# Four stacked graph layers on one core: a group's chain, weighing, sums and 11 of its 16 adds put into one slot, the rest into the next

## The reference

```
L0: msgs = edge_weight * h[src];  agg = segment_sum(msgs, dst);  leaky_relu((agg + h) @ W1.T + agg*h @ W2.T + b)
L1: a = <q[src], k[dst]> / sqrt(32) in 4 heads;  softmax over the edges of a dst;  agg = sum(sa * v[src]);  gate, norm
L2: two GATv2 layers (4 heads, then 1):  score = att . leaky_relu(xl[src] + xr[dst]);  softmax;  sum(alpha * xl[src])
L3: two typed layers (8 heads, 8 node types, 8 edge types):  a = <Watt k[src], q[dst]>;  softmax;  sum(alpha * Wmsg v[src])
```

## Time and profile before

| what | value |
| --- | --- |
| median of three runs | 6962.94 us |
| the profiled execution | 6951.92 us |
| its span | 6950.0 us |
| PE busy | 4911.1 us, 71% |
| DVE busy | 4761.2 us, 69% |
| POOL busy | 4755.9 us, 68% |
| ACT busy | 1562.0 us, 22% |
| mean granted PE clock | 0.786 |

### The profile page before, as it was taken

The page is one execution under the profiler, slowest core; times in us unless marked ns, Lnnn a source line. Parts: engine busy times, 40 slices in busy tenths (PEclk is TensorE's granted clock), DMA queues, the critical chain, the costliest instruction groups (busy, mean ns, idle before and its releaser), DMA issues. The chain is left out here.

```text
span 6950.0 us, 92236 instructions
## 1 busy us (share of the span) xinstructions
PE 4911.1 (71%) x26631; PEld 4085.5 (59%) x26631; DVE 4761.2 (69%) x14309; ACT 1562.0 (22%) x4929; POOL 4755.9 (68%) x5008
## 2 busy tenths in 40 slices
PE   2655555667766577777688888867888886667766
PEld 2444444556665465565466666656777775566665
DVE  4444443777877577877577777747777874788786
ACT  2433332222222111111112112111222221121121
POOL 3777776777776577777577666627777763777774
PEclk8666666777677788888799889968887886877776
DMA  4444445666666355555455555547766673666664
GB/s 133 165 164 158 159 164 146 204 216 210 214 217 180 125 161 167 166 155 167 121 171 179 167 164 175 168 121 228 242 229 229 231 219 134 215 226 220 223 226 138
DMA packets 408006, 1267.81 MB, mean 182 GB/s; under 512 B 128774, under 2 KB 189958, under 8 KB 321110
## 3 DMA queue, kind: packets, MB, share of 16 engines
q1 hardware_dynamic: 200000, 760.73, 30.7%
q0 software_dynamic: 200240, 496.31, 25.8%
q10 hardware_dynamic: 7270, 4.88, 0.3%
HBM read 1084.56 MB, written 176.98 MB: 182 GB/s over the span
## 5 line engine op out<-in xcount | busy, mean ns | idle before, releaser
L756 POOL DMA_INDIRECT gathered_rows<-table_l,arena x3056 | 2909.3, 952 | 1192.4 <-issue 904.2
L1298 PE MATMUL ps<-weighted_rows,onehot 128*128 128x136 f32 (+2 forms) x8320 | 1527.4, 341 | 573.9 <-DVE acc L1150 568.8
L1298 PEld LDWEIGHTS ps<-weighted_rows,onehot 128*128 128x128 f32 x8320 | 1353.3, 241 | 729.3 <-DVE weighted_rows L1139 334.1
L1260 PEld LDWEIGHTS ps<-dst_side,onehot_t 128*128 128x128 f32 x8320 | 1299.9, 232 | 384.1 <-issue 318.3
L756 POOL DMA_INDIRECT gathered_rows<-table_l,src_rel_edges x1120 | 1063.7, 950 | 603.5 <-issue 328.4
L1260 PE MATMUL ps<-dst_side,onehot_t 128*128 x8320 | 1381.4, 320 | 90.0 <-DVE products L1067 43.8
L1150 DVE TENSOR_TENSOR acc<-acc,ps 128x136 f32 (+2 forms) x4160 | 1185.9, 285 | 178.1 <-PE ps L1298 83.5
L1256 PE MATMUL ps<-gathered_rows,ident 128*128 128x512 f32 x832 | 547.3, 745 | 307.0 <-DMA gathered_rows<-table_l,arena 302.4
L1072 DVE TENSOR_REDUCE scores<-products 128x16 f32<-128x512 f32 (+2 forms) x1040 | 706.5, 679 | 10.0
L879 PE MATMUL ps<-gathered_rows,onehot 128*128 128x128 f32 x1664 | 346.3, 373 | 465.3 <-ACT gathered_rows L816 464.3
L756 POOL DMA_INDIRECT arena<-table_l,src_rel_edges x544 | 516.5, 950 | 180.2 <-issue 160.3
(11 more groups left out here) (322 smaller groups left out, 6029.5 us busy)
## 6 DMA issues: line engine op xcount, KB each, us to landing
onehot_t<-onehots_turned SPq DMA_DIRECT2D x260, 1024.0 KB
onehot<-onehots SPq DMA_DIRECT2D x260, 1024.0 KB
onehots<-onehot SPq DMA_DIRECT2D x52, 1024.0 KB, 6.8
onehots_turned<-onehot_t SPq DMA_DIRECT2D x52, 1024.0 KB, 4.3
table_l<-arena SPq DMA_DIRECT2D x50, 1024.0 KB
gathered_rows<-table_l,arena POOLq DMA_INDIRECT x3056, 2.5
segment_flags_sb<-segment_flags SPq DMA_DIRECT2D x1300, 8.2 KB
arena<-type_mask_rows SPq DMA_DIRECT2D x75, 256.0 KB
```

The source lines that it names most:

```text
L756: pool.indirect_dma_start(out=home(v, t // GC)[:, t % GC, :], out_offset=None, in_=table, in_offset=bass.IndirectOffsetOnAxis(ap=index[:, ...
L1260: ins = nc.tensor.matmul(ps[:, BZ + k, g * P:(g + 1) * P], e.ohT[:, u, t * P:(t + 1) * P], kRows[:, bass.ds(bs[t % 8], D)], start=not gat, ...
L1298: ins = nc.tensor.matmul(ps[:, BP + n % 3, at:at + PW], e.oh[:, u, t, :], exvT[:, t, :], start=True, stop=True)
```

## The change

VectorE's slot s now does, in this order: the last five adds of group s-2 around the scans of group s-1; the whole chain of s-1, with `product(s, 0)` and `score(s, 0)` in it; then a wait for the exponentials' columns of s-1 and its weighing; then the products and scores 1 to 3 of s with the first 11 adds (units 0 to 3) of s-1 between them. TensorE makes all four `dst_rows` of group s in slot s; those of chunks 2 and 3 stand behind `sums` 3 and 5. In the GAT passes the identity product comes after the four one-hot products instead of before them. There is one slot less at the end of a pass, and `first(k)` is 9 hooks earlier for blocks whose last tile is one of the first 8 or last 5 of its group (for tiles 8 to 10 it is 11 earlier). GpSimd does not gather the last two tiles, which hold no edges, and the waits on gathered rows are for that many fewer.

```diff
+ON_TIME = SUMMED[3][1]
...
+def rows_wanted(s, j, q):
+    return 64 * (q + 1) - (16 * LACK if s == NG - 1 and j == J - 1 else 0)
...
-            for t in range(GT):
+            for t in range(min(GT, NT_MAX - s * GT)):
...
# VectorE, slot(s): r = s - 1, o = s - 2
+                if late:
+                    bo = blocks_of(o, ON_TIME, GT - ON_TIME)
+                    unit_of_adds(o, 4, ON_TIME, bo)
                 if chain:
                     scan_tiles(r, v, rq)
+                if late:
+                    unit_of_adds(o, 5, ON_TIME, bo)
                 if chain:
                     turn_ends(r)
+                after.dve(dve, x)
                 after.dve(dve, x + 1)
...
                 if chain:
                     chain_backward(r, v)
                     hand_back_ends(r)
+                    open_drop(r)
+                    max_forward(r, v)
+                    max_backward(r, v)
+                    less_maximum(r)
+                if cur:
+                    score(s, 0)
                 after.dve(dve, x + 2)
                 if chain:
+                    e.excol_ready.wait(dve, a_no, r + 1)
+                    last_maxima(r)
+                    for j in range(J):
+                        weigh(r, (w - 1) % buffers, j)
+                    br = blocks_of(r, 0, ON_TIME)
+                    rescale(r, v, br[0])
                 after.dve(dve, x + 3)
                 if cur:
                     product(s, w, qw, 1)
                     score(s, 1)
+                if chain:
+                    unit_of_adds(r, 0, 0, br)
                 after.dve(dve, x + 4)
+                if chain:
+                    unit_of_adds(r, 1, 0, br)
                 after.dve(dve, x + 5)
                 if cur:
                     product(s, w, qw, 2)
                     score(s, 2)
+                if chain:
+                    unit_of_adds(r, 2, 0, br)
+                    unit_of_adds(r, 3, 0, br)
                 after.dve(dve, x + 6)
                 if cur:
                     product(s, w, qw, 3)
                     score(s, 3)
...
# TensorE, slot(s)
+                if chain:
+                    turn_scores(r)
                 after.pe(pe, x)
+                if cur:
+                    e.oht_here[u].wait(pe, a_no, 16 * (q + 1))
+                    dst_rows(s, w, qw, 0, bs)
+                after.pe(pe, x + 1)
+                if chain:
+                    spread_drop(r)
+                after.pe(pe, x + 2)
+                if chain:
+                    turn_back(r)
+                if cur:
+                    dst_rows(s, w, qw, 1, bs)
+                after.pe(pe, x + 3)
+                if chain:
+                    e.oh_here[v].wait(pe, a_no, 16 * (rq + 1))
+                    for n in range(3):
+                        sums(r, v, n)
...
+                after.pe(pe, x + 4)
+                if chain:
+                    sums(r, v, 3)
+                after.pe(pe, x + 5)
+                if cur:
+                    dst_rows(s, w, qw, 2, bs)
+                if chain:
+                    sums(r, v, 4)
+                    sums(r, v, 5)
+                after.pe(pe, x + 6)
+                if cur:
+                    dst_rows(s, w, qw, 3, bs)
                 after.pe(pe, x + 7)
...
-        return HOOKS * (s + 2) + 7 if t < 8 else HOOKS * (s + 3) + 1
+        return HOOKS * (s + 1) + 6 if t < ON_TIME else HOOKS * (s + 2)
```

More of the change, by code:

```diff
@@ L1047, in _ @@
             slot(NG, NG % ways, NG // ways, cur=False)
-            slot(NG + 1, (NG + 1) % ways, (NG + 1) // ways, cur=False, chain=False)
-            for x in range(HOOKS * (NG + 2), after.end):
+            for x in range(HOOKS * (NG + 1), after.end):
                 after.act(act, x)
@@ L1235, in _ @@
             for s in range(ways):
-                slot(s, s, 0, chain=s > 0, weighs=s > 1, late=s > 2)
+                slot(s, s, 0, chain=s > 0, late=s > 1)
             turns(slot, ways, NG, ways)
-            for n in range(3):
-                slot(NG + n, (NG + n) % ways, (NG + n) // ways, cur=False, chain=n < 1, weighs=n < 2)
-            for x in range(HOOKS * (NG + 3), after.end):
+            slot(NG, NG % ways, NG // ways, cur=False)
+            slot(NG + 1, (NG + 1) % ways, (NG + 1) // ways, cur=False, chain=False)
+            for x in range(HOOKS * (NG + 2), after.end):
                 after.dve(dve, x)
@@ L1331, in slot @@
                     dst_rows(s, w, qw, 3, bs)
-                after.pe(pe, x + 5)
-                after.pe(pe, x + 6)
-                if weighs:
-                    sums(p, u, 4)
-                    sums(p, u, 5)
-                if chain:
-                    turn_back(r)
-                if cur and ahead:
-                    un, un_q = two(wn, qn)
-                    e.oht_here[un].wait(pe, a_no, 16 * (un_q + 1))
-                    bn = blocks_of(s + 1, 0)
-                    dst_rows(s + 1, wn, qn, 0, bn)
@@ L1344, in slot @@
-                after.pe(pe, x + 7)
-                if cur:
-                    turn_scores(s)
-                if cur and ahead:
-                    dst_rows(s + 1, wn, qn, 1, bn)
-            e.oht_here[0].wait(pe, a_no, 16)
-            b0 = blocks_of(0, 0)
-            for j in range(2):
-                dst_rows(0, 0, 0, j, b0)
+                after.pe(pe, x + 7)
             for s in range(ways):
-                slot(s, s, 0, chain=s > 0, weighs=s > 1)
-            turns(slot, ways, NG - 1, ways)
@@ L1357, in _ @@
-            slot(NG - 1, (NG - 1) % ways, (NG - 1) // ways, ahead=False)
+                slot(s, s, 0, chain=s > 0)
+            turns(slot, ways, NG, ways)
             slot(NG, NG % ways, NG // ways, cur=False)
-            slot(NG + 1, (NG + 1) % ways, (NG + 1) // ways, cur=False, chain=False)
-            for x in range(HOOKS * (NG + 2), after.end):
+            for x in range(HOOKS * (NG + 1), after.end):
                 after.pe(pe, x)
```

121 lines of the change are left out of this document (35 added, 86 removed).

## The result

The changed kernel takes 7451.43 us in the median of 4 runs (7445.46 to 7455.41), the kernel before 6956.85 in the 4 runs beside it: a ratio of 1.0711, 95% interval 1.0691 to 1.0732. It is slower by 495 us; 7390 was forecast, 7040 to 7620 was the range. The profiled execution took 7455.41 us with a span of 7453.7, 503.5 above the one of before.

The account below looks back on a forecast made before the run. Gathers were taken to bound passes 1, 2 and 5 at 20.07 us a slot, but not 3 and 4. Longer slots lose 499 us, 72 are gained: 6951.9 + 499 - 72 = 7379, plus 11 gives 7390 us, range 7040 to 7620.

Parts of the forecast that it names:

- The bound: Passes 1, 2 and 5 run at the gathers' pace; slots may grow to 20.07 us free, excess counts 52 times.
- The two waits: VectorE waits before `product(s, 2)` 1.05 us and `product(s, 3)` 0.75 us a slot; GAT passes 0.95 more each.
- The half clock: TensorE at 1.2 GHz: slot 21.3 us instead of 18.2, GAT 27.4 instead of 20.3, weighted by each pass's share.
- the two chains: TensorE's `sums` 3 then `dst_rows` 2 before `product(s, 2)`; `sums` 5 then `dst_rows` 3 before `product(s, 3)`.
- the terms for after-work: Finished blocks' work: VectorE 0.9, 0.6, 1.0, 0.8, 0.9 us a slot by pass; TensorE 2.6 in pass 3.
- the after-work term of pass 4: Pass 4, TensorE: key and value with the query in one hook, another product of 16 matmuls; 2.8 us.
- The gain at the ends: Last score to last add at a pass's end: 18.5 us, 14 less than 32.5; five passes, 70 us.
- The identity products last: GAT passes' `dst_rows`: identity product lengthens both chains, 2 x 0.95 us a slot.
- What was to be seen: Profile signs: idle before chunk 2 and 3 products, weighing waiting for columns, GpSimd waiting nearly every slot, slower gathers.
- The waits do not fit into the slack: Rival, here denied: new waits fit the gathers' slack, slots of passes 1, 2, 5 stay 20.07; 6890 us, chance 0.10.
- full-speed costs alone: Rival: TensorE mostly at 2.4 GHz when its work is on the path; 153 us growth, about 7045, chance 0.10.
- the clock does not fall: Rival, here denied: more TensorE pauses, half speed a quarter of the time more; 312 us on top, 7700, chance 0.10.

Follow-up runs that it names:

- dst_early: Changed kernel with `dst_rows(2)` right behind `sums` 0 to 2 and `dst_rows(3)` ahead of `sums` 3 on TensorE: 6993.88 us, ratio 1.0068.
- rel_only: Changed kernel with TensorE's hook 0 behind `dst_rows(0)` and, in pass 4, ScalarE's relations copies ahead of its nine scaled copies: 7372.05 us, ratio 1.0606.
- dst2_only: Changed kernel with `dst_rows(2)` alone moved ahead of `sums` 3, `dst_rows(3)` staying behind `sums` 5: 7100.41 us, ratio 1.0216.
- ident_first: Changed kernel with the GATv2 passes' identity product ahead of the four dst products again: 7468.62 us, ratio 1.0756.

## Why the prediction was right, point by point

- **The bound.** Three passes at the gathers' pace, and a slot decides once it is above 20.07 us: dst_early shows it, coming down to 20.10, 20.37 and 20.12 in these passes and no further.
- **The two waits.** Forecast at 1.05 and 0.75 us, in GAT passes 0.95 more each, and more at half clock. Measured 1.13 to 1.23 and 0.33 to 0.84 in passes 1 and 5, 1.92 to 1.99 and 1.51 to 1.57 in passes 2 and 3. So the two together came at about the sizes counted for full clock, 1.8 and 3.7 us. Taking them away gave 458 us, 1.76 a slot over all passes; less than the waits themselves (2.73 a slot), since passes 1, 2 and 5 come down to the gathers' pace. This mechanism is the right one.
- **The half clock was put in the wrong place, and the sum came near in part by luck.** The prediction let the two chains run at half clock for 48, 30, 22, 36 and 48% of the time, as in the whole pass. That made 1.5, 2.1, 1.6, 1.1 and 1.5 us a slot; without it, its own count for full speed is 153 us of growth, not 499. (Doubled by its own rows, the first chain grows by 1.8, not 1.5.) In the changed kernel `dst_rows(2)` and `dst_rows(3)` take 1.05 to 1.11 us in the mean of each pass, at a granted clock of 0.98 to 1.00 (chunk 3 of pass 4: 1.32 at 0.86). The half clock lies on `dst_rows(1)`, behind the chain's pauses: 1.72 to 2.06 us at 0.50 to 0.69. Yet the slots grew by 607 us, so some 450 us stand elsewhere. Beside the two waits the trace has 130 us of adds that wait for sums and 154 of products 0 and 1 that wait for TensorE, over the five passes. Part of these lies in the terms for after-work, and how the 450 us divide wasn't told apart.
- **Other sizes that cancelled.** In pass 1 the slot is 0.4 above the forecast, in pass 3 0.7 below it. That is within the bounds given for the after-work; which piece is off wasn't told apart. The terms given for pass 4 add up to 22.9, not 22.8, and its slot before is 21.02 by the table's measure, not 20.8.
- **Pass 4 was mis-sized**: 25.66 for 22.8, 149 us. The step that failed is the after-work term of pass 4, "2.8 by the same count". It counted TensorE's instructions at pass 3's exposure. It did not count that TensorE's fourth `relations` waits for ScalarE, which has eight scaled copies (L2271) in front of the relations' copies, and that `dst_rows(0)`, or `turn_back` in 4 slots, stands behind it; placing that hook and these copies otherwise takes off 79 us (rel_only). Nor did it see that keys, values and query of a block in one hook (5.8 us) can come in front of `dst_rows(2)`; that is so in 5 slots, at most 29 of the 104 us by which dst2_only shortens the pass. In most long slots they come in front of `sums` 0 to 2, which the prediction counted in kind. What is left of the 149 us wasn't told apart. The clock over the slots of the pass was 0.82 before, 0.75 with these waits and 0.80 in rel_only.
- **The gain at the ends** was taken from pass 1 for all five, 14 us each. It was 14.7, 15.8, 20.9, 28.8 and 19.4, 99.6 instead of 70: the more after-work stood between the late adds before, the more there was to gain.
- **The identity products last** were given their length, 0.95, in both chains, and no price for the place; ident_first shows none.
- **What was to be seen**: GpSimd waits for the weighing 181 times in 260 slots, not in nearly every one, and the columns are waited for (0.73 and 0.17 in the slot shown). The gathers were to take 1100, 1200 and 1300 us in passes 1 to 3 and take 1093.0, 1135.4 and 1206.6: they run ahead, so the slots, not they, carry the loss.
- **The rivals.** The waits do not fit into the slack (all slots above 20.07); full-speed costs alone, 7045, are too few, although the two chains did run at nearly full clock; the clock does not fall (0.86 in pass 2, where 0.70 was the mark), except in pass 4.
- **The sum.** The slots grew by 607 us instead of 499, the ends gave 30 more, and the median lies 4 us below the profiled execution, not 11 above it: +108 - 30 - 15 = 63, of the 61 between 7390 and 7451.
